# Batch 0 of the last loop: half of the quad sums on GpSimd, and the order of residuals and squares

## The chip, the cores and the metric

The kernel is one program on one core of a Trainium2 chip. The core has five engines that run side by side and meet only at semaphores: TensorE (PE, matrix products), VectorE (DVE), ScalarE (ACT), GpSimd (POOL) and SyncE (SP, which here only starts transfers). Transfers between the large memory and the core's own memory (SBUF) run on 16 DMA engines; they are started from SP and from ACT. The metric is the device time of one execution in microseconds (us), as the median of several runs.

## The reference

`x` is (8, 128, 256, 256) float32. Two layers are computed:

```python
x = x + _L0_conv_ref(_gn(x), ...)   # layer 0
x = x + _L1_conv_ref(_gn(x), kernel)  # layer 1: 4x4 depthwise blur of the group-normed x
# layer 0, inside:
ll, lh, hl, hh = haar_dwt(x)                     # to half resolution, 4*128 channels
h = gelu(batchnorm(conv1x1(cat(ll, lh, hl, hh), w_c1, b_c1)))       # 128 channels
o = dwconv3x3(h, dw_w, dw_b); o = layernorm_chw(o); o = conv1x1(o, pw1)
h = conv1x1(gelu(o), pw2) + h                                       # u below
h = gelu(batchnorm(conv1x1(h, w_c2, b_c2)))      # 4*128 channels: LL, LH, HL, HH
# haar_idwt: y00 = (ll+lh+hl+hh)/2, y01 = (ll+lh-hl-hh)/2, y10 = (ll-lh+hl-hh)/2, y11 = (ll-lh-hl+hh)/2
```

## The kernel before

Channels lie on the 128 partitions. The program has three stages. The first reads `x` for statistics and makes the first 1x1 convolution. The second makes the depthwise and pointwise convolutions and leaves `u_scratch`. The third, `phase_tail`, starts its first x load at 2587.4 us and is the only one that the change touches.

`phase_tail` works on units. A unit is 8 image rows of one batch, 32 units to a batch. For each unit `k` of batch `b`:

- SP (`load_unit`) loads `u_in` (256 KB) and the matching piece of `x` into one of four slots of `x_tile` (1024 KB). A slot is loaded again when the `y` stored from it four units earlier has landed.
- PE (`convolve`, L1289) makes four products of 128x512, one for each Haar band, into the PSUM tiles `conv_psum` 0 to 3. Each float32 product shows as two MATMUL records.
- ACT (`gelus`, L1397) applies batch norm and gelu: bands 0 and 2 to `gelu_out` (two buffers), bands 1 and 3 in place in PSUM.
- DVE (`pairs`, L1162) makes four pair sums of 128x512, each from one SBUF and one PSUM operand, into `pair_sums`, which has one buffer. Its semaphore also frees PSUM bands 1 and 3 for PE.
- DVE (`quads`, L1170) makes two quad sums of 128x1024 from `pair_sums`, both operands in SBUF: the one with ADD gives the even columns of `quad_sums`, the one with SUBTRACT the odd columns. Each row is written with a step of two elements.
- DVE (`residual`, L1177) makes `x_tile = 0.5 * quad_sums + x_tile` over 128x2048, both in SBUF.
- ACT (`finish`) starts the store of the `x_tile` slot to `y_scratch` (L1404, 1024 KB) and squares the slot for the second group norm (L1408).

Batch `b-1` is blurred beside the units of batch `b`. `split` on ACT makes `y_hi` and `y_centred_tile`, `rests` on GpSimd (L1106) makes `y_lo`, `blur` on PE multiplies both with band matrices, and `take` on DVE (L1184, one PSUM and one SBUF operand) adds the result to `y_tile`. The body is written out for the phases FIRST (batch 0), SECOND (batch 1), MIDDLE (a hardware loop over batches 2 to 7), DRAIN and END. In FIRST there is nothing to blur, and GpSimd has no instruction. The order on each engine is the order in which the Python code writes it. In every phase up to MIDDLE the order on DVE is pairs(k), quads(k), residual(k), and on ACT gelus(k), finish(k-1).

`y_tile` has eight slots of 128x2048. In FIRST none of them is in use; the first loads into them are made in SECOND.

Of the kernel before, what the change touches and what calls it, by code (L numbers as in the profile page):

```python
# [8 lines left out]
ALU = mybir.AluOpType  # L9
# [5 lines left out]
H2, W2 = H // 2, W // 2  # L15
# [871 lines left out]
UNITS = H // ROWS3  # L887
# [16 lines left out]
FIRST, SECOND, MIDDLE, DRAIN, END = range(5)  # L904


def group_at(b, phase, k, lag):

    if phase == FIRST or (phase == SECOND and k < lag) or (phase == END and k >= lag):
        return None  # L910
    return b * NG - NG + (k - lag)


def phase_tail(nc, kp, wc2, x, u_d, y_d, out):
# [4 lines left out]
    with ExitStack() as ctx:  # L919
        sb = lambda name, shape, dt=F32: ctx.enter_context(nc.sbuf_tensor(name, shape, dt))  # L920
        ps = lambda name, shape: ctx.enter_context(nc.psum_tensor(name, shape, F32))
        sem = kp["sem"]
        w = sb("w_conv2", [128, 4 * C])
# [6 lines left out]
        x_t = sb("x_tile", [128, XS, XW])  # L930
        u_t = sb("u_in", [128, US, UW])
        g_t = sb("gelu2_out", [128, 2, 2, UW])
        sums_t = sb("pair_sums", [128, 4, UW])
        d_t = sb("quad_sums", [128, XW])
# [3 lines left out]
        y_t = sb("y_tile", [128, YS, 2, GRP, W])  # L938
# [12 lines left out]
        spread_s = sb("gn2_seam_spread", [128, 2, NQ])  # L951
        rest_n = sb("rests_of_partition", [128, 1])
        rest_i = sb("rests", [1, 1], mybir.dt.int32)
        cv = [ps(f"conv2_psum{s}", [128, BANK]) for s in range(4)]
        bl = [ps(f"blur_psum{t}", [128, GRP, W]) for t in range(2)]
        small = cv[2]
# [12 lines left out]
        s_ge = sem("gelu2_done")  # L969
        s_s1 = sem("pair_sums_done")  # L970
        s_s2 = sem("quad_sums_done")
        s_y = sem("y_ready")
        s_sq = sem("y_squared")
        s_yst = [sem(f"y_stored{i}") for i in range(XS)]
# [26 lines left out]
        yr = y_d.rearrange("b c h w -> (b c) h w")  # L1001
        ov = out.rearrange("b c h w -> (b c) h w")
        block = ctx.enter_context(nc.Block())

        def phases(engine, body):
            body(0, FIRST)
# [77 lines left out]
        @block.gpsimd  # L1084
        def _(pool):

            for y in (y_hi, y_lo):
                for cols in (slice(0, 2), slice(2 + W, PADW)):
                    pool.memset(y[:, :, :, cols].bitcast(F32), 0.0).then_inc(s_set, 1)
            for y in (seam_hi, seam_lo):  # L1090
                for cols in (slice(0, 2), slice(2 + W, PADW)):
                    pool.memset(y[:, cols].bitcast(F32), 0.0).then_inc(s_set, 1)
            pool.wait_ge(s_v, 5)
            nc.gpsimd.tensor_tensor(t4[:, 2, :], t4[:, 1, :], neg_half[:, 0:4], ALU.pow).then_inc(s_rs, 1)

            def rests(b, phase, k):
                g = k - LAG_SPLIT
                h = g % 2
                at = b * NG - NG + g
                pool.wait_ge(s_hi, at + 1)  # L1100
                pool.wait_ge(s_c, at + 1)
                if not (phase == SECOND and g < 2):
                    pool.wait_ge(s_t, 2 * at - 2)
                for t in range(2):
                    part = slice(t * GRP, (t + 1) * GRP)
                    nc.gpsimd.tensor_tensor(  # L1106
                        y_lo[:, h, part, 2:2 + W], y_c[:, part, :],
                        y_hi[:, h, part, 2:2 + W].bitcast(F32), ALU.subtract).then_inc(s_lo, 1)
                if g % QUAD == 2:
                    pool.wait_ge(s_sc, b * NQ - NQ + g // QUAD + 3)  # L1110
                    nc.gpsimd.tensor_tensor(seam_lo[:, 2:2 + W], seam_c[:],
                                            seam_hi[:, 2:2 + W].bitcast(F32), ALU.subtract).then_inc(s_slo, 1)

            def body(b, phase):
                for k in range(LAG_SPLIT if phase == END else UNITS):
                    if group_at(b, phase, k, LAG_SPLIT) is not None:
                        rests(b, phase, k)
                    if k == 1 and SECOND <= phase <= DRAIN:
                        pool.wait_ge(s_gve, b)
                        nc.gpsimd.tensor_tensor(st[:, 8:9], st[:, 7:8], neg_half[:, 0:1], ALU.pow).then_inc(s_grs, 1)  # L1120

            phases(pool, body)

        @block.vector
        def _(dve):
# [28 lines left out]
            dve.wait_ge(s_p, 5)  # L1154
            nc.vector.tensor_copy(rest_i[:], cv[0][0:1, 0:1]).then_inc(s_ready, 1)

            def pairs(b, k):
                for p in range(2):

                    dve.wait_ge(s_ge, b * (4 * UNITS) + 4 * k + 2 * p + 2 + 4)  # L1160
                    for m, op in enumerate((ALU.add, ALU.subtract)):
                        ins = nc.vector.tensor_tensor(sums_t[:, 2 * m + p, :], g_t[:, k % 2, p, :], cv[2 * p + 1][:], op)  # L1162
                    ins.then_inc(s_s1, 1)

            def quads(b, k):
# [4 lines left out]
                    ins = nc.vector.tensor_tensor(dv[:, :, e], sv[:, :, 0], sv[:, :, 1], op)  # L1170
                ins.then_inc(s_s2, 1)

            def residual(b, k):
                i = k % XS
                dve.wait_ge(s_x[i], b * (16 * UNITS // XS) + 16 * (k // XS) + 16)
                dve.wait_ge(s_s2, b * UNITS + k + 1)
                nc.vector.scalar_tensor_tensor(x_t[:, i, :], d_t[:], 0.5, x_t[:, i, :],  # L1177
                                               ALU.mult, ALU.add).then_inc(s_y, 1)

            def take(b, k, t):  # L1180
# [14 lines left out]
            def body(b, phase):  # L1195
                c = b - 1
                done = SECOND <= phase <= DRAIN
                gl = Chain(dve, s_gl, c * LINKS_GN)
                for k in range(LAG_BLUR if phase == END else UNITS):
                    if phase <= MIDDLE:  # L1200
                        pairs(b, k)
                    if done and k == 1:

                        dve.wait_ge(s_sq, b * UNITS + XS)
# [17 lines left out]
                        ins.then_inc(s_gsp, 1)  # L1222
                    if phase <= MIDDLE:
                        quads(b, k)
                        residual(b, k)
                    if done and k == 1:
                        dve.wait_ge(s_gp, b * 2 - 1)
                        gl.link(nc.vector.tensor_copy(st[:, 5:6], small[:, 0:1]))
# [15 lines left out]
                    if group_at(b, phase, k, LAG_BLUR) is not None:  # L1244
# [3 lines left out]
                        take(b, k, 1)  # L1248

            phases(dve, body)  # L1250

        @block.tensor
# [126 lines left out]
        def _(act):  # L1379
# [20 lines left out]
            def finish(b, k):  # L1400

                i = k % XS
                act.wait_ge(s_y, b * UNITS + k + 1)
                act.dma_start(yv[bass.ds(b, 1), :, k * XW:(k + 1) * XW].rearrange("b c n -> c (b n)"),  # L1404
                              x_t[:, i, :]).then_inc(s_yst[i], 16)

                act.wait_ge(s_sq, b * UNITS + k + XS)
                nc.scalar.activation(junk[:], x_t[:, i, :], ACT.Square, bias=neg_gm[:, bass.ds(b, 1)],  # L1408
                                     accum_out=y_sq[:, bass.ds(b, 1), k]).then_inc(s_sq, 1)
# [31 lines left out]
            def body(b, phase):  # L1441
                for k in range(LAG_SPLIT if phase == END else UNITS):
                    if phase <= MIDDLE:
                        gelus(b, k)
                    if k >= 1 and phase <= MIDDLE:
                        finish(b, k - 1)
                    elif k == 0 and SECOND <= phase <= DRAIN:
                        finish(b - 1, UNITS - 1)
                    if group_at(b, phase, k, LAG_SPLIT) is not None:
                        split(b, phase, k)  # L1450
                        if (k - LAG_SPLIT) % QUAD == 2:
                            split_seam(b, phase, k)
# [50 lines left out]
```

## Time and profile before

| | |
|---|---|
| median of 3 runs | 5678.01 us (5661.07 to 5681.14) |
| the profiled execution's own time | 5670.85 us |
| its span in the trace | 5669.0 us |
| TensorE's mean granted clock | 0.97 of full speed |
| FIRST, first unit's pair sums to batch 1's first pair sums | 2603.59 to 2834.11 us |
| busy over the span: PE, DVE, ACT, POOL | 92%, 77%, 66%, 36% |

The span runs from the first to the last record of the trace; the execution's own time is 1.85 us longer. Shares of busy time are means over three stages and say little about one of them. For FIRST the stretch from 2600 to 2834 us has to be read by itself.

### The profile page before, as it was taken

How to read it: one execution, taken by the hardware profiler on the slowest of the kernel's cores; microseconds unless marked ns; L12 is line 12 of the kernel's file. 1: busy time of each engine (PE TensorE's matmuls, PEld its weight loads, DVE VectorE, ACT ScalarE, POOL GpSimd, SP SyncE). 2: the span in 40 equal slices, each digit the busy share in tenths (PEclk: the TensorE clock that was granted, in tenths of full speed). 3: DMA queues.
4: the chain of work that ended last, by engine and by line, in shares of the span. 5: the costliest groups of instructions: out<-in, count | busy, mean ns of one | idle time of the engine just before them, and what ended most of it. 6: DMA issues, size and time to landing. Idle time of an engine off the chain costs nothing. (4 is left out here: it accounts for less than half of the span.)

```text
span 5669.0 us, 67162 instructions
## 1 busy us (share of the span) xinstructions
PE 5201.0 (92%) x18136; PEld 3151.9 (56%) x18136; DVE 4380.2 (77%) x5325; ACT 3721.8 (66%) x5012; POOL 2066.9 (36%) x1397
## 2 busy tenths in 40 slices
PE   2888888986999999997699999999999999999999
PEld 1333333332555555563256666676666666666777
DVE  8555555428999999966988888888888888888833
ACT  0333333346777777755678787787887878878744
POOL 0000000018777777730023333333333333333354
PEclk9999999998999999998899999999999999999999
DMA  9999999842333333326999999999999999999986
GB/s 369 375 374 377 379 378 375 343 142 72 107 110 108 107 106 106 108 86 240 330 384 404 396 399 401 390 399 383 389 394 388 399 389 398 398 392 393 397 291 228
DMA packets 829594, 1729.83 MB, mean 305 GB/s; under 512 B 50064, under 2 KB 587152, under 8 KB 718608
## 3 DMA queue, kind: packets, MB, share of 16 engines
q1 hardware_dynamic: 755472, 1389.81, 66.6%
q10 hardware_dynamic: 73728, 335.58, 14.4%
q8 instruction: 148, 2.42, 0.2%
q14 instruction: 246, 2.02, 0.1%
HBM read 1050.95 MB, written 674.23 MB: 304 GB/s over the span
## 5 line engine op out<-in xcount | busy, mean ns | idle before, releaser
L1106 POOL TENSOR_TENSOR y_lo<-y_centred_tile,y_hi 128x1024 fp32r<-128x1024 f32 x512 | 1040.8, 2054 | 1724.5 <-ACT y_centred_tile L1427 1410.4
L1306 PE MATMUL blur_psum<-y_hi,band_hi 128*128 128x512 f32 x4096 | 1127.8, 417 | 8.8 <-DVE y_tile L1184 7.4
L1289 PE MATMUL conv_psum<-u_in,w_conv 128*128 128x512 f32 x2048 | 971.2, 618 | 109.1 <-DVE pair_sums L1162 85.2
L1306 PE MATMUL blur_psum<-y_lo,band_hi 128*128 128x512 f32 x4096 | 1041.8, 396 | 7.5 <-POOL y_lo L1106 7.0
L1306 PEld LDWEIGHTS blur_psum<-y_hi,band_hi 128*128 128x128 f32 x4096 | 764.9, 188 | 278.8 <-issue 100.9
L1162 DVE TENSOR_TENSOR pair_sums<-gelu_out,conv_psum 128x512 f32<-128x512 f32 x1024 | 653.5, 684 | 305.7 <-ACT conv_psum L1397 299.8
L1306 PEld LDWEIGHTS blur_psum<-y_lo,band_hi 128*128 128x128 f32 x4096 | 769.4, 188 | 200.7 <-POOL y_lo L1106 16.5
L1184 DVE SCALAR_TENSOR_TENSOR y_tile<-blur_psum,rstd_all,y_tile 128x1024 f32<-128x1024 f32 x512 | 639.6, 1277 | 159.4 <-PE blur_psum L1306 152.2
L1397 ACT ACTIVATE gelu_out<-conv_psum,bn_shift,bn_scale 128x512 f32<-128x512 f32 x512 | 397.5, 776 | 515.3 <-PE conv_psum L1289 493.7
L1289 PEld LDWEIGHTS conv_psum<-u_in,w_conv 128*128 128x128 f32 x2048 | 398.1, 197 | 559.7 <-issue 407.1
L608 POOL TENSOR_TENSOR tap_products<-tap_products 128x512 f32<-128x512 f32 x512 | 653.8, 1277 | 43.0 <-ACT tap_products L869 6.5
L869 ACT ACTIVATE tap_products<-h_ring,vectors 128x512 f32<-128x512 f32 x768 | 499.0, 712 | 215.0 <-POOL depthwise_out L612 215.0
L313 DVE BATCH_NORM_STATS2 x_stats<-x_resident 128x6 f32<-128x512 f32 x640 | 395.2, 681 | 294.7 <-DMA x_resident<-x 293.5
L1170 DVE TENSOR_TENSOR quad_sums<-pair_sums 128x1024 f32<-128x1024 f32 x512 | 604.8, 1223 | 8.4
L1177 DVE SCALAR_TENSOR_TENSOR x_tile<-quad_sums,x_tile 128x2048 f32<-128x2048 f32 x256 | 596.9, 2332 | 13.9
L1425 ACT ACTIVATE y_hi<-y_tile,neg_mean_all 128x2048 fp32r<-128x2048 f32 x256 | 513.3, 2005 | 137.6 <-POOL y_lo L1106 137.6
L374 PE MATMUL z_psum<-x_resident,w_folded 128*128 128x512 f32 x1280 | 600.1, 625 | 0.5 <-ACT z_psum L399 0.5
L657 DVE SCALAR_TENSOR_TENSOR dw_psum<-h_ring,vectors,dw_psum 128x512 f32<-128x512 f32 x768 | 578.0, 753 | 25.2 <-PE dw_psum L761 6.7
L395 ACT ACTIVATE z_tile<-z_psum,z_bias 128x512 f32<-128x512 f32 x256 | 176.0, 687 | 638.5 <-DMA z_scratch<-z_tile 428.3
L761 PE MATMUL dw_psum<-h_ring,tap_diagonals 128*128 128x512 f32 x1024 | 500.9, 612 | 65.3 <-DVE depthwise_out L657 54.9
L1408 ACT ACTIVATE junk<-x_tile,neg_group_mean 128x2048 bf16<-128x2048 f32 x256 | 511.7, 1999 | 59.8 <-DVE x_tile L1177 56.6
L1427 ACT ACTIVATE y_centred_tile<-y_tile,neg_mean_all 128x2048 f32<-128x2048 f32 x256 | 509.7, 1991 | 0.0
(166 smaller groups left out, 5451.4 us busy)
## 6 DMA issues: line engine op xcount, KB each, us to landing
x_tile<-x SPq DMA_DIRECT2D x256, 1024.0 KB, 10.0
y_scratch<-x_tile ACTq DMA_DIRECT2D x256, 1024.0 KB, 8.4
y_tile<-y_scratch SPq DMA_DIRECT2D x512, 512.0 KB, 10.9
out<-y_tile SPq DMA_DIRECT2D x512, 512.0 KB, 10.1
x_stream<-x SPq DMA_DIRECT2D x192, 1024.0 KB, 11.4
x_resident<-x SPq DMA_DIRECT2D x160, 1024.0 KB, 11.1
z_scratch<-z_tile ACTq DMA_DIRECT2D x256, 256.0 KB, 7.2
z_in<-z_scratch SPq DMA_DIRECT2D x256, 256.0 KB, 2.8
```

The source lines that it names most:

```text
L374: ins = nc.tensor.matmul(zp[q % ZP][:, half * BANK:(half + 1) * BANK], w_f[:, p, :], px[:, p // 2, p % 2, rows, :], start=(p == 0), stop=( ...
L608: nc.gpsimd.tensor_tensor(pr[:, 0, :], pr[:, 0, :], pr[:, n, :], ALU.add).then_inc(s_add, 1)
L657: taps.link(nc.vector.scalar_tensor_tensor(to.rearrange("p (r c) -> p r c", c=W2), tap(k, e), V[:, V_DWW + k:V_DWW + k + 1], acc.rearrange ...
L1106: nc.gpsimd.tensor_tensor(y_lo[:, h, part, 2:2 + W], y_c[:, part, :], y_hi[:, h, part, 2:2 + W].bitcast(F32), ALU.subtract).then_inc(s_lo, 1)
L1162: ins = nc.vector.tensor_tensor(sums_t[:, 2 * m + p, :], g_t[:, k % 2, p, :], cv[2 * p + 1][:], op)
L1170: ins = nc.vector.tensor_tensor(dv[:, :, e], sv[:, :, 0], sv[:, :, 1], op)
L1177: nc.vector.scalar_tensor_tensor(x_t[:, i, :], d_t[:], 0.5, x_t[:, i, :], ALU.mult, ALU.add).then_inc(s_y, 1)
L1184: nc.vector.scalar_tensor_tensor(y_t[:, g % YS, t], bl[t][:], rs_b[:, bass.ds(n, 1)], y_t[:, g % YS, t], ALU.mult, ALU.add).then_inc(s_ev, 1)
L1289: nc.tensor.matmul(cv[s][:], w[:, s * C:(s + 1) * C], u_t[:, k % US, :], start=True, stop=True).then_inc(s_mm, 1)
L1306: ins = nc.tensor.matmul(bl[t][:, 2 * c:2 * c + 2, :], wt[:, kw, :], y[:, h, ch:ch + 2, kw:kw + W], start=(m == 0 and kw == 0), stop=(m == ...
L1408: nc.scalar.activation(junk[:], x_t[:, i, :], ACT.Square, bias=neg_gm[:, bass.ds(b, 1)], accum_out=y_sq[:, bass.ds(b, 1), k]).then_inc(s_s ...
L1425: nc.scalar.activation(y_hi[:, h, :, 2:2 + W], src, ACT.Identity, bias=nm_b[:, bass.ds(n, 1)]).then_inc(s_hi, 1)
```

## The change

Only FIRST changes. The steps are:

1. GpSimd makes the odd quad sums of batch 0's 32 units. DVE makes the even ones (`even_quads`) and then signals `quad_sums_done`; GpSimd waits for that and signals `odd_sums_done`.
2. `pair_sums` and `quad_sums` get a second buffer each, in the unused slots 4 and 5 of `y_tile`; units alternate between them.
3. DVE's order becomes pairs(k), residual(k-1), even_quads(k). Before residual(k-1) it waits for `odd_sums_done` of unit k-1. After unit 31 there is one more residual by itself.
4. ACT's order becomes gelus(k), finish(k-2), with finish(30) added at the end of FIRST; finish(31) stays in SECOND, behind the gelus of batch 1's first unit.

```diff
+        sums_of = [sums_t[:], y_t[:, 4].rearrange("p t c w -> p (t c w)").rearrange("p (s n) -> p s n", s=4)]
+        quads_of = [d_t[:], y_t[:, 5].rearrange("p t c w -> p (t c w)")]
...
+        s_q1 = sem("odd_sums_done")
...
+        def quad_views(k):
+            dv = quads_of[k % 2].rearrange("c (i a j e) -> c a e i j", a=2, e=2, j=W2)
+            sv = sums_of[k % 2].rearrange("c (a p) (i j) -> c a p i j", p=2, j=W2)
+            return dv[:, :, 0], dv[:, :, 1], sv[:, :, 0], sv[:, :, 1]
...
 @@ gpsimd, body(b, phase)
+                    if phase == FIRST:
+                        pool.wait_ge(s_s2, k + 1)
+                        _, odd, first, second = quad_views(k)
+                        nc.gpsimd.tensor_tensor(odd, first, second, ALU.subtract).then_inc(s_q1, 1)
...
 @@ vector
+            def even_quads(k):
+                dve.wait_ge(s_s1, 2 * k + 2 + 4)
+                even, _, first, second = quad_views(k)
+                nc.vector.tensor_tensor(even, first, second, ALU.add).then_inc(s_s2, 1)
...
+                if phase == FIRST:
+                    for k in range(UNITS + 1):
+                        if k < UNITS:
+                            pairs(0, k, sums_of[k % 2])
+                        if k >= 1:
+                            dve.wait_ge(s_q1, k)
+                            residual(0, k - 1, quads_of[(k - 1) % 2])
+                        if k < UNITS:
+                            even_quads(k)
+                    return
...
 @@ scalar, body(b, phase)
-                    if k >= 1 and phase <= MIDDLE:
+                    if phase == FIRST:
+                        if k >= 2:
+                            finish(b, k - 2)
+                        if k == UNITS - 1:
+                            finish(b, k - 1)
+                    elif k >= 1 and phase <= MIDDLE:
                         finish(b, k - 1)
```

How this moves instructions is shown by what stands in a row on an engine. First VectorE at the start of the last loop, before (L1162 is pairs, L1170 quads, L1177 residual; conv2_psum is what the trace calls conv_psum):

```order
L1162 TENSOR_TENSOR pair_sums<-gelu2_out,conv2_psum1 128x512 x2
L1162 TENSOR_TENSOR pair_sums<-gelu2_out,conv2_psum3 128x512 x2
L1170 TENSOR_TENSOR quad_sums<-pair_sums 128x2x4x128 x2
L1177 SCALAR_TENSOR_TENSOR x_tile<-quad_sums,x_tile 128x2048
L1162 TENSOR_TENSOR pair_sums<-gelu2_out,conv2_psum1 128x512 x2
```

and the same place now (L1176 is pairs, L1191 even_quads, L1197 residual; y_tile is the second buffer):

```order
L1176 TENSOR_TENSOR pair_sums<-gelu2_out,conv2_psum1 128x512 x2
L1176 TENSOR_TENSOR pair_sums<-gelu2_out,conv2_psum3 128x512 x2
L1191 TENSOR_TENSOR quad_sums<-pair_sums 128x2x4x128
L1176 TENSOR_TENSOR y_tile<-gelu2_out,conv2_psum1 128x512 x2
L1176 TENSOR_TENSOR y_tile<-gelu2_out,conv2_psum3 128x512 x2
L1197 SCALAR_TENSOR_TENSOR x_tile<-quad_sums,x_tile 128x2048
L1191 TENSOR_TENSOR y_tile<-y_tile 128x2x4x128
L1176 TENSOR_TENSOR pair_sums<-gelu2_out,conv2_psum1 128x512 x2
```

Each unit has one quad sum instead of two on VectorE, and a unit's residual stands behind the next unit's pair sums.

At the end of FIRST, where batch 1 begins, VectorE has now:

```order
L1191 TENSOR_TENSOR quad_sums<-pair_sums 128x2x4x128
L1176 TENSOR_TENSOR y_tile<-gelu_out,conv_psum 128x512 x4
L1197 SCALAR_TENSOR_TENSOR x_tile<-quad_sums,x_tile 128x2048
L1191 TENSOR_TENSOR y_tile<-y_tile 128x2x4x128
L1197 SCALAR_TENSOR_TENSOR x_tile<-y_tile,x_tile 128x2048
L1176 TENSOR_TENSOR pair_sums<-gelu_out,conv_psum 128x512 x4
L1184 TENSOR_TENSOR quad_sums<-pair_sums 128x2x4x128 x2
```

The last residual of batch 0 follows its quad sum with no pair sums between the two; from L1184 on the order is the old one.

## Rows read from the trace of the kernel before

**Rows 1.** The page's busy times over the whole span

```profile
PE 5201.0 (92%) x18136; PEld 3151.9 (56%) x18136; DVE 4380.2 (77%) x5325; ACT 3721.8 (66%) x5012; POOL 2066.9 (36%) x1397
```

**Rows 2.** Windows of batch 0's units, of loops before and behind; columns as in the first line

```profile
core 0: us, PE busy (x) PEld busy (x) DVE busy (x) ACT busy (x) POOL busy (x), PEclk, DMA share, GB/s
700.00:800.00 100.00, 93.34 (x196) 38.74 (x197) 56.76 (x92) 33.23 (x85) 0.00 (x0) 0.93 0.99 397
...
2740.00:2780.00 40.00, 26.69 (x45) 10.54 (x46) 39.27 (x41) 27.83 (x40) 0.00 (x0) 0.83 0.91 319
3000.00:3100.00 100.00, 100.00 (x377) 69.58 (x376) 86.85 (x84) 81.62 (x85) 36.00 (x20) 1.00 1.05 404
```

**Rows 3.** Timeline of one unit of FIRST: start us, length us, engine, line, operation

```profile
2709.73 2.29 DVE L1177 SCALAR_TENSOR_TENSOR x_tile<-quad_sums,x_tile 128x2048 f32<-128x2048 f32 x1
2711.94 2.47 DVE L1162 TENSOR_TENSOR pair_sums<-gelu_out,conv_psum 128x512 f32<-128x512 f32 x4
...
2712.44 2.00 ACT L1408 ACTIVATE junk<-x_tile,neg_group_mean 128x2048 bf16<-128x2048 f32 x1 [2.35 <-DVE x_tile L1177]
...
2713.27 3.70 PE L1289 MATMUL conv_psum<-u_in,w_conv 128*128 128x512 f32 x8 [3.48 <-DVE pair_sums L1162]
...
2714.45 2.38 DVE L1170 TENSOR_TENSOR quad_sums<-pair_sums 128x1024 f32<-128x1024 f32 x2
...
2716.53 0.75 ACT L1397 ACTIVATE conv_psum<-conv_psum,bn_shift,bn_scale 128x512 f32<-128x512 f32 x1
2716.93 2.29 DVE L1177 SCALAR_TENSOR_TENSOR x_tile<-quad_sums,x_tile 128x2048 f32<-128x2048 f32 x1
```

**Rows 4.** Durations by line: pairs, quads (whole trace), residuals, products; min/median/max ns

```profile
L1162 DVE TENSOR_TENSOR pair_sums<-gelu_out,conv_psum x122: 680/681/684, 2612.5 to 2828.7; 128x512 f32<-128x512 f32 x122
...
L1170 DVE TENSOR_TENSOR quad_sums<-pair_sums x512: 1216/1225/1249, 2606.6 to 5365.8; 128x1024 f32<-128x1024 f32 x171
...
L1177 DVE SCALAR_TENSOR_TENSOR x_tile<-quad_sums,x_tile x32: 2291/2292/2293, 2609.1 to 2831.9; 128x2048 f32<-128x2048 f32 x32
...
L1289 PE MATMUL conv_psum<-u_in,w_conv x248: 592/592/1222, 2612.6 to 2831.4; 128*128 128x512 f32 x124
```

**Rows 5.** Timeline of VectorE: batch 0's first quad sums, batch 1's first pair sums

```profile
2606.63 2.36 DVE L1170 TENSOR_TENSOR quad_sums<-pair_sums 128x1024 f32<-128x1024 f32 x2
...
2834.11 2.47 DVE L1162 TENSOR_TENSOR pair_sums<-gelu_out,conv_psum 128x512 f32<-128x512 f32 x4
```

**Rows 6.** Durations of GpSimd's two-input subtraction, whole trace; min/median/max ns

```profile
L1106 POOL TENSOR_TENSOR y_lo<-y_centred_tile,y_hi x512: 1987/2000/4047, 2868.4 to 5655.4; 128x1024 fp32r<-128x1024 f32 x171
```

**Rows 7.** Timeline: one hand-over from VectorE to GpSimd, one back

```profile
2304.91 0.75 DVE L657 SCALAR_TENSOR_TENSOR depthwise_out<-h_ring,vectors,dw_psum 128x512 f32<-128x512 f32 x1
...
2305.81 1.27 POOL L612 TENSOR_TENSOR depthwise_out<-depthwise_out,tap_products 128x512 f32<-128x512 f32 x1 [0.37 <-DVE depthwise_out L657]
...
2596.22 1.02 POOL L1094 TENSOR_TENSOR four_columns<-four_columns,neg_half 128x4 f32<-128x4 f32 x1 [9.21 <-DVE four_columns L1145]
...
2597.28 0.17 DVE L1151 TENSOR_TENSOR bn_scale<-four_columns,vectors 128x4 f32<-128x4 f32 x1 [0.33 <-POOL four_columns L1094]
```

**Rows 8.** Timeline: y_lo beside pairs, and y_lo beside a residual, last loop

```profile
2868.40 3.97 POOL L1106 TENSOR_TENSOR y_lo<-y_centred_tile,y_hi 128x1024 fp32r<-128x1024 f32 x2 [17.99 <-ACT y_centred_tile L1427]
...
2869.67 2.62 DVE L1162 TENSOR_TENSOR pair_sums<-gelu_out,conv_psum 128x512 f32<-128x512 f32 x4 [1.12 <-ACT conv_psum L1397]
...
3210.78 6.65 POOL L1106 TENSOR_TENSOR y_lo<-y_centred_tile,y_hi 128x1024 fp32r<-128x1024 f32 x2 [6.07 <-ACT y_centred_tile L1427]
3211.60 3.97 DVE L1177 SCALAR_TENSOR_TENSOR x_tile<-quad_sums,x_tile 128x2048 f32<-128x2048 f32 x1
```

**Rows 9.** DMA issues in FIRST: KB each, median us from issue to landing

```profile
y_scratch<-x_tile ACTq DMA_DIRECT2D x32, 1024.0 KB, 6.2
x_tile<-x SPq DMA_DIRECT2D x31, 1024.0 KB, 6.3
u_in<-u_scratch SPq DMA_DIRECT2D x32, 256.0 KB, 5.3
```

More of the change, by code:

```diff
@@ L1155, in _, with pairs @@
             nc.vector.tensor_copy(rest_i[:], cv[0][0:1, 0:1]).then_inc(s_ready, 1)
-            def pairs(b, k):
+            def pairs(b, k, sums):
                 for p in range(2):
@@ L1161, in pairs @@
                     for m, op in enumerate((ALU.add, ALU.subtract)):
-                        ins = nc.vector.tensor_tensor(sums_t[:, 2 * m + p, :], g_t[:, k % 2, p, :], cv[2 * p + 1][:], op)
+                        ins = nc.vector.tensor_tensor(sums[:, 2 * m + p, :], g_t[:, k % 2, p, :], cv[2 * p + 1][:], op)
                     ins.then_inc(s_s1, 1)
@@ L1171, in quads, with residual @@
                 ins.then_inc(s_s2, 1)
-            def residual(b, k):
+            def even_quads(k):
+                dve.wait_ge(s_s1, 2 * k + 2 + 4)
+                even, _, first, second = quad_views(k)
+                nc.vector.tensor_tensor(even, first, second, ALU.add).then_inc(s_s2, 1)
+            def residual(b, k, quads):
                 i = k % XS
@@ L1176, in residual @@
                 dve.wait_ge(s_s2, b * UNITS + k + 1)
-                nc.vector.scalar_tensor_tensor(x_t[:, i, :], d_t[:], 0.5, x_t[:, i, :],
+                nc.vector.scalar_tensor_tensor(x_t[:, i, :], quads, 0.5, x_t[:, i, :],
                                                ALU.mult, ALU.add).then_inc(s_y, 1)
@@ L1198, in body @@
                 gl = Chain(dve, s_gl, c * LINKS_GN)
+                if phase == FIRST:
[8 more added lines that the diff above has]
+                    return
                 for k in range(LAG_BLUR if phase == END else UNITS):
                     if phase <= MIDDLE:
-                        pairs(b, k)
+                        pairs(b, k, sums_t)
                     if done and k == 1:
@@ L1224, in body @@
                         quads(b, k)
-                        residual(b, k)
+                        residual(b, k, d_t[:])
                     if done and k == 1:
```

## The prediction, made before the changed kernel ran

> **What bounds the kernel now.** I began with the page's busy times [rows 1]: PE is busy for 92% of the span and DVE for 77%. That would say that relief for DVE is worth nothing, but it is a mean over three stages. The windows [rows 2] take it apart. From 3000 to 3100 us PE is busy for all of the time; from 2740 to 2780 us, in FIRST, DVE is busy for 39.27 of 40 us and PE for 26.69. The timeline of one unit [rows 3] then shows who waits for whom. DVE runs residual (2709.73), pairs (2711.94), quads (2714.45), residual (2716.93) with no idle time noted, while PE waits 3.48 us for pair_sums and ACT 2.35 us for x_tile. So DVE alone sets the pace. One unit takes 2716.93 - 2709.73 = 7.20 us, and from the first quad sums to batch 1's first pair sums [rows 5] it is 2834.11 - 2606.63 = 227.48 us for 31 steps from unit to unit and one end. That stretch is what I forecast; the loops before and behind keep their instructions.
>
> **DVE's unit after the change.** I use steps from start to start, not lengths, since the instructions overlap. Residual to pairs is 2711.94 - 2709.73 = 2.21 us [rows 3]. Four pairs end 2.47 us after their start and one lasts 0.68 us [rows 3, 4], so one step is (2.47 - 0.68) / 3 = 0.60 and four are 2.39 us. Two quads end after 2.38 us and one lasts 1.23 [rows 3, 4], so one step is 1.15 us. Before, quads begin 2.51 us after pairs and residual 2.48 us after quads; both contain about 0.1 to 0.2 us in which DVE waits for its own last result. In the new order neither residual(k-1) nor even_quads(k) needs the instruction right in front of it, so these gaps go too. DVE's own unit is 2.39 + 2.21 + 1.15 = 5.75 us. Removed: one quad of 1.15 to 1.24 us and 0.2 to 0.3 us of gaps.
>
> **The new wait.** Residual(k-1) waits for GpSimd's odd sum. Behind it on DVE stand even_quads(k) and pairs(k+1), for which PE and ACT wait. The loop is: even sum 1.23 [rows 4]; hand-over to GpSimd 0.15 (L657 ends at 2305.66, L612 starts at 2305.81 [rows 7]); odd sum D; hand-over back 0.04 (2597.24 to 2597.28 [rows 7]); residual 2.21. That is 3.63 + D. No row shows GpSimd writing with a step of two elements. The nearest has the same shape and operand count, y_lo, with a median of 2.00 us, a lowest value of 1.99 and a longest of 4.05 [rows 6]. 1.99 and 4.05 are my ends, and I take 2.00, since elements and operands are the same. The loop is then 5.63 us, hidden under DVE's 5.75 by 0.12 us. If D were over 2.12 us each further 0.1 us would cost 0.1 us a unit.
>
> **Does GpSimd disturb DVE?** At 3210.78 two y_lo need 6.65 us together instead of 3.97, and the residual that starts among them at 3211.60 lasts 3.97 us instead of 2.29 [rows 4, 8]. So GpSimd and a residual hold each other up. In the new order they cannot meet: residual waits for the odd sum, and the odd sum for the even one. What runs beside the odd sum is pairs, with one operand in PSUM. From 2869.67 to 2872.29 four pairs ran beside two y_lo: 2.62 us for the pairs instead of 2.47, and 3.97 us for the two y_lo, as elsewhere. I take nothing, and carry the 0.15 us, which for a unit on DVE's pace would make 5.90 us, inside the next term. The Trainium skill (SBUF — State Buffer, section "SBUF: two separate sides") calls the port pair an exclusive lock between GpSimd and DVE work with two SBUF inputs, held for the whole instruction. That speaks against handing a sum to GpSimd beside a busy DVE; by its wording pairs stay outside the lock, and the sum by it is the same as by rows 8, which agree.
>
> **ACT and PE.** ACT's unit is square to last gelu, 2712.44 to 2717.28, or 4.84 us [rows 3], and about 0.4 us for the store issue: 5.2 us, under 5.75. The store of unit k-1 is issued behind gelus(k+1); those end close to the end of residual(k-1), so the store is not later than now by more than some tenths. PE's four products take 3.70 us at full clock [rows 3]. From the end of pairs(k) the band-3 product (0.93) and gelu (0.75) need 1.7 us, and pairs(k+1) wants them after 2.21 + 1.15 + 1.20 = 4.6 us: 2.9 us of slack. But the granted clock is 0.83 there [rows 2], that is, for a third of the time at 1.2 GHz instead of 2.4, and a product's record then lasts 1222 instead of 592 ns [rows 4]. A unit that falls wholly into it needs 1.2 + 1.2 us for each of three products behind pairs' first half, 7.3 + 0.75 - 1.2 = 6.9 us, 2.3 us late. Spells are mostly shorter than a unit, so I carry 0 to 0.1 us a unit, inside the next term.
>
> **The DMA engines.** This is what is late next. A unit moves 1024 + 1024 + 256 KB [rows 9] = 2.36 MB, at 7.20 us 328 GB/s. At 5.75 us it would be 410 GB/s. The fastest long stretches are 404 GB/s at a share of 1.05 and 397 GB/s at 0.99 [rows 2]. In FIRST a share of 0.91 carried only 319 GB/s; scaled to 1.05 that is 368. So the unit is bounded by 2.36/404 = 5.84 us on one side and 2.36/368 = 6.41 us on the other. The ends are near each other and I take the middle, 6.1 us. Latency does not bind: store and load have medians of 6.2 and 6.3 us [rows 9], with the residual some 15 us against 4 x 6.1 = 24 us for four slots.
>
> **Sum.** 31 x 6.1 + 3.63 + 2.00 = 194.7 us; the last part is the end of FIRST, where even sum, odd sum and residual stand one behind the other with nothing between, and costs 5.63 us once. Saved: 227.48 - 194.7 = 32.8 us. Against the profiled execution's own 5670.85 us (span 5669.0) this gives 5638 us. That execution is 7 us under the median of the runs, 5678.01, and between the fastest, 5661.07, and it; I keep its level. With the ends 5.84 and 6.41 us the saving is 40.8 and 23.2 us: 5630 and 5648.
>
> **Rivals.**
> - DVE's own pace holds, DMA follows at 410 GB/s: 31 x 5.75 + 5.63 = 183.9, 43.6 us saved, 5627 us. For it: DVE is the only engine without idle time. Against: no long window reached 410. Chance 0.20.
> - The DMA engines saturate as soon as their share is 1.00 at FIRST's own yield: 319/0.91 = 351 GB/s, 6.73 us a unit, 214.3 us, 13 us saved, 5658 us. For it: the poor yield in FIRST. Against: shares of 1.05 and 404 GB/s. Chance 0.14. The Trainium skill (SBUF — State Buffer, section "A bandwidth-pool intuition that's wrong (but worth ruling out)") gives about 358 GB/s between HBM and a core; an estimate by it is 6.59 us a unit and 5653 us. The trace's 404 GB/s over 100 us disagrees.
> - TensorE's low clock catches whole units, one in three late by the 2.3 us above: 6.5 us a unit, 207 us, 20 us saved, 5650 us. For it: 0.83. Against: PE and ACT have slack, and the spells now cost DVE nothing. Chance 0.08.
> - Slower: the odd sum on GpSimd is slow, by its stepped writes or because pairs do shut it out. It decides from D = 227.48/32 - 3.63 = 3.48 us. At the longest 4.05 us [rows 6] the unit is 7.68 us, 245.8 us in all, 18 us lost, 5689 us. For it: one operation of unknown write pattern. Against: a median of 2.00 us in 512 cases. Chance 0.06.
> - The saving appears in FIRST and batch 1 gives it back, since its y loads and gn2 columns wait for batch 0's last stores and squares: 5670 us. Against: these are in the same distance from the last residual as now. Chance 0.04.
>
> **How the numbers follow.** The forecast (5.84 to 6.41 us a unit) has 0.48. What a measurement of this kernel can tell from no change is about 0.5%, 28 us. The forecast passes that up to 6.25 us a unit, about four fifths of its chance, 0.38; with the first rival, faster is 0.58. The rest of the forecast and the second, third and fifth rival are 0.36; slower 0.06. The range runs from 5627 less some scatter, 5621, to the second rival's 5658 and some scatter, 5664.
>
> **What would show it.** In the changed profile: batch 0's residuals 5.8 to 6.4 us apart; GpSimd's new line at 2.0 to 2.1 us, starting 0.15 us behind the even sum; DVE with small idle times put down to x loads, where the DMA share is about 1.05; no idle time before residual put down to GpSimd. The forecast is wrong if residual waits for GpSimd in each unit, if DVE waits for ACT's gelus in most, or if the distance stays near 7.2 us.

## The result

| kernel | median, us | runs | ratio to the kernel before, 95% interval |
|---|---|---|---|
| before | 5669.81 (5657.97 to 5681.14) | 13 | |
| changed | 5656.42 (5651.93 to 5669.07) | 13 | 0.998 (0.9973 to 0.9988) |

The change saves 13 us, a gain that is clear of noise, and I had forecast 33. The time lies inside my range, but the gain is only 0.4 of the forecast one. The page and the rows below come from the slowest of the 13 executions (5669.07 us); a second trace is read near the end of the experiments.

The page's first lines of the changed kernel:

```profile
span 5667.0 us, 67162 instructions
...
PE 5208.1 (92%) x18136; PEld 3155.5 (56%) x18136; DVE 4342.4 (77%) x5293; ACT 3725.1 (66%) x5012; POOL 2141.6 (38%) x1429
```

VectorE has 38 us less work than in [rows 1] (4342.4 against 4380.2) and GpSimd 75 us more (2141.6 against 2066.9). So the work moved as intended. These are the windows of batch 0, columns as in [rows 2]:

```profile
2680.00:2720.00 40.00, 25.65 (x40) 10.00 (x40) 30.47 (x33) 25.70 (x36) 13.02 (x6) 0.74 0.87 317
2720.00:2760.00 40.00, 25.87 (x49) 10.16 (x50) 34.74 (x36) 29.40 (x43) 14.80 (x7) 0.91 0.93 344
```

In these two windows DVE is busy for 30.47 and 34.74 of 40 us, where it was busy for 39.27 [rows 2]. DVE got less to do and in part just idles. The DMA engines are at a share of 0.87 and 0.93, about as before (0.91); whether they could carry more can't be read from these rows, and the experiments have to say it. The durations, as in [rows 4] and [rows 6]:

```profile
L1129 POOL TENSOR_TENSOR quad_sums<-pair_sums x16: 2354/2363/2383, 2608.9 to 2813.9; 128x1024 f32<-128x1024 f32 x16
...
L1197 DVE SCALAR_TENSOR_TENSOR x_tile<-quad_sums,x_tile x16: 2284/2285/2293, 2611.3 to 2821.4; 128x2048 f32<-128x2048 f32 x16
```

The odd sum takes 2.36 to 2.37 us and not the 2.00 of y_lo. Next come one unit of the changed kernel that does not run as planned (from 2697.30 us) and one that does (from 2720.64 us). The lines are from the timeline of DVE and GpSimd, with one of PE's products; the bracket is the idle time before, and who ended it:

```profile
2697.30 2.29 DVE L1197 SCALAR_TENSOR_TENSOR x_tile<-y_tile,x_tile 128x2048 f32<-128x2048 f32 x1
...
2700.41 9.81 PE L1319 MATMUL conv_psum<-u_in,w_conv 128*128 128x512 f32 x16 [7.22 <-DMA u_in<-u_scratch]
...
2705.01 1.28 DVE L1176 TENSOR_TENSOR y_tile<-gelu_out,conv_psum 128x512 f32<-128x512 f32 x2 [4.29 <-ACT conv_psum L1427]
...
2708.82 2.29 DVE L1197 SCALAR_TENSOR_TENSOR x_tile<-quad_sums,x_tile 128x2048 f32<-128x2048 f32 x1
...
2720.64 2.29 DVE L1197 SCALAR_TENSOR_TENSOR x_tile<-quad_sums,x_tile 128x2048 f32<-128x2048 f32 x1
...
2722.85 1.22 DVE L1191 TENSOR_TENSOR y_tile<-y_tile 128x1024 f32<-128x1024 f32 x1
...
2723.99 2.48 DVE L1176 TENSOR_TENSOR pair_sums<-gelu_out,conv_psum 128x512 f32<-128x512 f32 x4
2724.15 2.37 POOL L1129 TENSOR_TENSOR y_tile<-y_tile 128x1024 f32<-128x1024 f32 x1 [3.54 <-DVE y_tile L1191]
...
2726.55 2.29 DVE L1197 SCALAR_TENSOR_TENSOR x_tile<-y_tile,x_tile 128x2048 f32<-128x2048 f32 x1
```

From 2720.64 to 2726.55 residuals are 5.91 us apart. GpSimd's sum starts at 2724.15 and ends at 2726.52, and the residual starts at 2726.55: it waits for GpSimd. At 2697.30 and 2708.82 they are 11.52 us apart. There DVE stood idle for 4.29 us in the middle of its pair sums, waiting for ACT, because PE had stood idle for 7.22 us for u_in. These are the waits of batch 0 (engine, line, whom for: us in total, times, longest):

```profile
PE conv_psum L1319 <- DMA u_in<-u_scratch: 67.5, 22, 7.2
...
ACT gelu_out L1427 <- PE conv_psum L1319: 63.7, 27, 17.2
DVE y_tile L1176 <- ACT conv_psum L1427: 32.1, 22, 4.3
```

Before, PE waited in the same stretch for DVE's pair_sums and never for u_in:

```profile
PE conv_psum L1289 <- DVE pair_sums L1162: 81.8, 31, 3.9
```

From the first quad sum (2607.57) to batch 1's first pair sums (2829.52) it is 221.95 us, against 227.48 [rows 5]. The 31 distances between residuals lie between 5.89 and 11.52 us and are 6.97 in the mean; before, all were 7.18 to 7.20.

**Where the u_in load hangs.** The same place with SP and ACT (SPq and ACTq are DMA issues):

```profile
2688.93 0.33 SPq L1034 DMA_DIRECT2D x_tile<-x  x1
...
2689.42 0.34 ACTq L1434 DMA_DIRECT2D y_scratch<-x_tile  x1
...
2690.09 1.99 ACT L1438 ACTIVATE junk<-x_tile,neg_group_mean 128x2048 bf16<-128x2048 f32 x1
...
2692.20 0.33 SPq L1029 DMA_DIRECT2D u_in<-u_scratch  x1
...
2697.91 0.33 SPq L1034 DMA_DIRECT2D x_tile<-x  x1
2698.28 0.43 SPq L1029 DMA_DIRECT2D u_in<-u_scratch  x1
```

The square that starts at 2690.09 ends at 2692.1, and at 2692.20 SP issues the u_in load: `load_unit` waits for `y_squared` of unit k-4 before it loads u_in for unit k. The load lands 8.2 us later and PE starts at 2700.41. The next u_in load was free by its square at about 2696.9, but SP stood at the x load before it, which waits for the y store of 2689.42 to land, until 2697.91; u_in followed at 2698.28. The diff does not touch `load_unit`. But it moves the squares and the stores a unit back against the gelus, and both are what SP waits for. The kernel had this wait on `y_squared` before the change too; the description of `load_unit` ahead of the prediction leaves it out.

### The profile page after: what moved, and what is told of

Same layout as the page of the kernel before. It is cut to its first block and busy times, and to the rows that moved or that the text cites. A ratio compares the mean times of both kernels' runs of the same rounds, so it can differ in the third digit from the quotient of the medians.

```text
span 5667.0 us, 67162 instructions
## 1 busy us (share of the span) xinstructions
PE 5208.1 (92%) x18136; PEld 3155.5 (56%) x18136; DVE 4342.4 (77%) x5293; ACT 3725.1 (66%) x5012; POOL 2141.6 (38%) x1429
## 5 line engine op out<-in xcount | busy, mean ns | idle before, releaser
L1176 DVE TENSOR_TENSOR pair_sums<-gelu_out,conv_psum 128x512 f32<-128x512 f32 x960 | 614.2, 684 | 308.7 <-ACT conv_psum L1427 308.6
L1197 DVE SCALAR_TENSOR_TENSOR x_tile<-quad_sums,x_tile 128x2048 f32<-128x2048 f32 x240 | 560.2, 2334 | 11.0
L1184 DVE TENSOR_TENSOR quad_sums<-pair_sums 128x1024 f32<-128x1024 f32 x448 | 529.1, 1223 | 7.3
## 6 DMA issues: line engine op xcount, KB each, us to landing
out<-y_tile SPq DMA_DIRECT2D x512, 512.0 KB, 10.4
```

What stands on the lines that cost most here:

```text
L1176: ins = nc.vector.tensor_tensor(sums[:, 2 * m + p, :], g_t[:, k % 2, p, :], cv[2 * p + 1][:], op)
L1197: nc.vector.scalar_tensor_tensor(x_t[:, i, :], quads, 0.5, x_t[:, i, :], ALU.mult, ALU.add).then_inc(s_y, 1)
```

## The experiments

Theory A: the u_in load now hangs on a square and a store that come later, so load, products, gelus and square form a loop that is longer than DVE's unit. Rival B: the DMA engines cannot carry a unit's 2.36 MB faster. Rival C: TensorE's low clock makes the products late. "Stretch" is always from the first quad sum to batch 1's first pair sums, "distance" the mean of the 31 distances between residuals; both are read from VectorE's timeline of each run.

| kernel | distance, us | stretch, us | time, us |
|---|---|---|---|
| before | 7.19 | 227.48 | 5669.81 (13 runs) |
| changed | 6.97 | 221.95 | 5656.42 (13 runs) |
| changed, a second trace | 6.66 | 212.26 | 5663.65 (one) |
| u_in waits for the product, old place | 6.75 | 214.99 | 5655.16 (6 runs) |
| u_in one unit ahead, waits for the square | 6.40 | 204.32 | 5651.34 (one) |
| u_in one unit ahead, waits for the product | 6.05 | 193.37 | 5636.76 (4 runs) |
| u_in two units ahead, waits for the product | 5.91 | 189.23 | 5635.87 (4 runs) |
| the same, even sum ahead of the residual | 5.81 | 190.14 | 5628.18 (4 runs) |

**u_in one unit ahead, waiting for the product.** In batch 0 SP loads u_in for k+1 before it waits for x's slot of unit k:

```diff
-                sp.wait_ge(s_sq, b * UNITS + k + 1)
-                sp.dma_start(u_t[:, k % US, :], ...).then_inc(s_u[k % US], 16)
+                def load_u(m):
+                    if m >= US:
+                        sp.wait_ge(s_mm, 4 * (m - US) + 4 + 16)
+                    sp.dma_start(u_t[:, m % US, :], ...).then_inc(s_u[m % US], 16)
+                if phase == FIRST:
+                    if k == 0:
+                        load_u(0)
+                    if k + 1 < UNITS:
+                        load_u(k + 1)
+                    sp.wait_ge(s_sq, k + 1)
...
```

From batch 1 on the u_in load stays as it was.

> The changed kernel, with one edit in batch 0: SP issues the load of u_in for unit k+1 ahead of unit k's x load, and it waits for the product of unit k-3 and no longer for a square. In the changed kernel residuals are 6.97 us apart in the mean and PE waits some 60 us for u_in. Theory A (the u_in load hangs on the square, which now comes one unit later, so load, products, gelus, square form a loop): the wait of PE for u_in goes, residuals are 5.9 to 6.1 us apart, batch 0 takes 187 to 195 us from its first quad sum to batch 1's first pair sums, the time falls to 5625 to 5640 us. Rival B (the 16 DMA engines can't carry 2.36 MB in under about 6.7 us here): the wait only moves to the x loads, residuals stay 6.6 to 7.0 us apart, the time stays within 8 us of the changed kernel's. Rival C (TensorE's low clock makes the products late): waits of ACT and DVE for products remain, 6.5 us or more.

Measured: 0.9935 (0.9918 to 0.9952) of the kernel before, 5636.76 us, distance 6.05, stretch 193.37 us. PE's waits in batch 0 are now:

```profile
PE conv_psum L1333 <- DMA u_in<-u_scratch: 33.7, 16, 5.8
```

Distance, stretch and time are what theory A gave. Its "the wait goes" came only half true: 33.7 us of 67.5 are left. B and C as the cause of the 6.97 us fall: the same bytes are carried, and the same products made, in 6.05 us a unit. The median is 20 us lower than that of the changed kernel. C has a part all the same. These are PE's products of two units in a row, in the changed kernel:

```profile
2655.22 5.09 PE L1319 MATMUL conv_psum<-u_in,w_conv 128*128 128x512 f32 x8 [3.81 <-DMA u_in<-u_scratch]
2661.63 3.70 PE L1319 MATMUL conv_psum<-u_in,w_conv 128*128 128x512 f32 x8 [1.31 <-DMA u_in<-u_scratch]
```

The granted clock is 0.82 from 2620 to 2700 us, between 1.2 and 2.4 GHz by turns. In this trace a unit's products that meet the lower one last 5.1 to 5.4 us instead of 3.70. As long as PE waits for u_in they stand in the loop of theory A and lengthen it. How much of the 6.97 us that makes was not separated.

**The two halves of that edit.** Only the semaphore, in the old place on SP:

```diff
+                if phase == FIRST:
+                    if k >= US:
+                        sp.wait_ge(s_mm, 4 * (k - US) + 4 + 16)
+                else:
                     sp.wait_ge(s_sq, b * UNITS + k + 1)
                 sp.dma_start(u_t[:, k % US, :], ...).then_inc(s_u[k % US], 16)
+                if phase == FIRST:
+                    sp.wait_ge(s_sq, k + 1)
```

> The changed kernel, with the u_in load of batch 0 waiting for the product of unit k-4 instead of the square, but in its old place on SP, behind the x load of unit k-1, which waits for the y store of unit k-5. Theory A: a longer loop is left (gelus(k-3), y store 7.0 us, x load issued, u_in 6.4 us, products and gelus 4.4 us: 18 us for 3 units): 6.0 to 6.4 us apart, and time 5630 to 5648 us, between the changed kernel and the one with u_in ahead. Rival B: as the changed kernel, 6.6 to 7.0 us.

Measured: 0.9974 (0.9961 to 0.9986), 5655.16 us, distance 6.75, stretch 214.99 us: as the changed kernel. That is what rival B gave and a miss for theory A's 6.0 to 6.4 us. My 18 us for the loop through the store were too few; in this run SP waited 163 us in all for y stores. Only the order, with the wait for the square kept:

```diff
                     if m >= US:
-                        sp.wait_ge(s_mm, 4 * (m - US) + 4 + 16)
+                        sp.wait_ge(s_sq, m + 1)
```

> The changed kernel with u_in of unit k+1 issued ahead of x of unit k in batch 0, but still behind the square of unit k-3. The kernel with the product's semaphore and the old place brought 6.75 us between residuals, the one with both edits 6.05. Theory A has two loops: one through the square (store issue and square 2.7, u_in 6.4, products and gelus 4.4 us: 13.5 us for two units, 6.75 us), one through the y store in front of it on SP (about 18 us for three units and more with waits). With the square's wait kept, the first loop stays: 6.6 to 7.1 us apart, stretch 210 to 225 us, PE waits 40 us or more for u_in. Rival: if SP's order alone was the cause, 6.0 to 6.2 us.

Measured: distance 6.40, stretch 204.32 us, 5651.34 us in a single run. Its waits:

```profile
PE conv_psum L1333 <- DMA u_in<-u_scratch: 59.9, 26, 5.0
```

The distance is between both expectations and a miss for either. With this trace's median landing of 5.8 us instead of 6.4 the loop through the square gives (2.7 + 5.8 + 4.4) / 2 = 6.45 us, close to the 6.40. It is one trace, and the stretches of the changed kernel's two traces differ by 10 us (221.95 and 212.26). Still, with either wait left in place the distance stays at 6.40 or more, against 6.05 without both: both have to go.

**The same edit in the kernel before.**

> The kernel before, with the u_in load of batch 0 ahead in the same way. All theories: PE never waited for u_in there, DVE sets the pace; residuals stay 7.19 us apart and batch 0's stretch 227 to 228 us. If it gets shorter, the u_in load already cost something before.

Measured: distance 7.18, stretch 227.35 us, 5673.90 us in a single run. The u_in load cost nothing as long as DVE took 7.19 us.

**u_in two units ahead.**

```diff
                     if k == 0:
                         load_u(0)
-                    if k + 1 < UNITS:
-                        load_u(k + 1)
+                        load_u(1)
+                    if k + 2 < UNITS:
+                        load_u(k + 2)
```

> The changed kernel with u_in in batch 0 loaded two units ahead of x instead of one. With one unit ahead residuals were 6.05 us apart in the mean (25 of 31 at 5.9) and PE still waited 34 us for u_in. Theory A (the rest was the u_in load too): 5.91 to 5.95 us apart, batch 0's stretch 189 to 190 us, 3 to 4 us less than with one ahead, time 5630 to 5637 us. Rival B (the DMA engines are full at a share of 0.99): the 6.05 us stay, and the waits show up at x loads.

Measured: 0.9938 (0.9921 to 0.9955), 5635.87 us, distance 5.91 with no exception, stretch 189.23 us. Its u_in loads, with the time to landing:

```profile
L1031 SPq DMA_DIRECT2D u_in<-u_scratch x26: 327/734/1832, 2603.4 to 2757.8; - x26
...
DMA to landing us min/median/max: 3.5/10.4/12.7
```

The same window in the kernel before and in this one, columns as in [rows 2]:

```profile
2610.00:2780.00 170.00, 108.83 (x189) 42.10 (x190) 166.78 (x167) 116.77 (x166) 0.00 (x0) 0.86 0.88 319
...
2610.00:2780.00 170.00, 116.43 (x223) 44.63 (x222) 167.24 (x174) 142.54 (x199) 68.80 (x29) 0.92 1.00 389
```

Its waits of PE:

```profile
PE conv_psum L1334 <- DVE pair_sums L1191: 26.4, 15, 2.2
PE conv_psum L1334 <- DVE y_tile L1191: 26.2, 15, 2.2
...
PE conv_psum L1334 <- DMA u_in<-u_scratch: 3.7, 1, 3.7
```

PE waits for u_in once, for 3.7 us. The u_in load now takes a median of 10.4 us to land, and but for that once nobody waits. The DMA engines move 389 GB/s at a share of 1.00, against 319 at 0.88 in the same window of the kernel before: B falls for good.

**The even sum ahead of the residual**, so that the residual meets GpSimd's sum:

```diff
-                        if k >= 1:
-                            dve.wait_ge(s_q1, k)
-                            residual(0, k - 1, quads_of[(k - 1) % 2])
                         if k < UNITS:
                             even_quads(k)
+                        if k >= 1:
+                            dve.wait_ge(s_q1, k)
+                            residual(0, k - 1, quads_of[(k - 1) % 2])
```

> As the one with u_in two units ahead, and on VectorE the even sum(k) stands in front of residual(k-1) instead of behind it, so that the residual can meet the odd sum(k). If GpSimd and a two-SBUF-input instruction of VectorE shut each other out and VectorE is first, the odd sum starts only when the residual ends, 2.2 us later than now, and runs beside the pair sums; the unit is then 1.15 + 2.21 + 2.39 = 5.75 us up to 5.9 us, batch 0's stretch 184 to 189 us. If GpSimd is first each time, the residual lasts 4.6 us or starts 2.4 us late and the unit is 8.1 to 8.3 us, stretch 260 us. If they did not disturb each other, the odd sum would start 0.1 us behind the even sum, with 5.75 us a unit.

Measured: 0.9928 (0.9909 to 0.9948), 5628.18 us, the fastest median of all, though its interval overlaps the one above. One unit of it (timeline of DVE and GpSimd):

```profile
2716.88 2.28 DVE L1212 SCALAR_TENSOR_TENSOR x_tile<-quad_sums,x_tile 128x2048 f32<-128x2048 f32 x1
2717.05 4.36 POOL L1144 TENSOR_TENSOR y_tile<-y_tile 128x1024 f32<-128x1024 f32 x1 [1.50 <-DVE y_tile L1206]
...
2719.09 2.47 DVE L1191 TENSOR_TENSOR pair_sums<-gelu_out,conv_psum 128x512 f32<-128x512 f32 x4
...
2721.59 1.23 DVE L1206 TENSOR_TENSOR quad_sums<-pair_sums 128x1024 f32<-128x1024 f32 x1
...
2722.74 2.29 DVE L1212 SCALAR_TENSOR_TENSOR x_tile<-y_tile,x_tile 128x2048 f32<-128x2048 f32 x1
2722.90 4.36 POOL L1144 TENSOR_TENSOR quad_sums<-pair_sums 128x1024 f32<-128x1024 f32 x1 [1.50 <-DVE quad_sums L1206]
```

The residual starts in front of GpSimd's sum and keeps its 2.28 us. The sum's record is 4.36 us long instead of 2.37. It ends at 2721.41, 2.25 us after the residual (2719.16), so it looks as if the sum stood still while the residual ran and then worked beside the pair sums. The expectation had it start later; the record starts at once and is longer. The unit is 2722.74 - 2716.88 = 5.86 us. The 0.11 us over DVE's own 5.75 are the gap between pairs and the even sum, which again stands right behind them (2721.59 - 2719.09 = 2.50 us instead of 2.39). GpSimd's sum is off the path, since it has until after the next even sum. The stretch is no shorter than the 189.23 us above. At its end PE waits 10.5 us for batch 1's first u_in load, and the last residual and batch 1's first pair sums are 5.20 us apart (2779.95 to 2785.15) instead of 2.21; at its start the first residual comes 1.1 us later. So the two traces of batch 0 don't show the 8 us between the medians.

**GpSimd's sum in the old order.** DVE keeps pairs, even sum, wait, residual; ACT finishes one unit behind, by the same edit as in the next experiment:

```diff
+                    for k in range(UNITS):
+                        pairs(0, k, sums_of[k % 2])
+                        even_quads(k)
+                        dve.wait_ge(s_q1, k + 1)
+                        residual(0, k, quads_of[k % 2])
```

> The changed kernel, in which DVE and ACT keep the old order: pairs(k), even sum(k), wait for the odd sum, residual(k), and finish one unit behind the gelus. The odd sum (2.37 us in the changed kernel) then stands in DVE's row: 2.39 + 1.22 + 0.08 + 2.37 + 0.03 + 2.21 = 8.3 us a unit, batch 0's stretch 262 to 268 us, 35 to 40 us more than the kernel before. Rival: if GpSimd and DVE disturbed each other beyond that, or not at all, it would be 9 us or more, or near 7.2.

Measured: distance 8.41, stretch 266.63 us, 5715.31 us. The residual waits 2.46 us for GpSimd in each unit, so it has to stand behind the next unit's pair sums. In this run VectorE does nothing beside the odd sum:

```profile
L1129 POOL TENSOR_TENSOR quad_sums<-pair_sums x16: 2344/2350/2357, 2610.2 to 2862.5; 128x1024 f32<-128x1024 f32 x16
```

It lasts 2.35 us even so. The pair sums beside it are thus not the reason for its length in the changed kernel.

**ACT's old order in the changed kernel.**

```diff
-                    if phase == FIRST:
-                        if k >= 2:
-                            finish(b, k - 2)
-                        if k == UNITS - 1:
-                            finish(b, k - 1)
-                    elif k >= 1 and phase <= MIDDLE:
+                    if k >= 1 and phase <= MIDDLE:
```

> The changed kernel with ACT's old order: store and square of unit k-1 behind the gelus of unit k, as before. The square then waits for residual(k-1), which now stands behind pairs(k); gelus(k+1) stand behind the square, and pairs(k+1) wait for them: 2.39 + 0.2 + 2.29 + 0.5 + 2.1 + 1.6 = 9.1 us a unit, 8.8 to 9.3, batch 0's stretch 278 to 292 us, 50 to 65 us more than the kernel before. So the two-unit lag, whatever it does to the u_in load, is what makes the rest possible. Rival: if the lag were not needed, 5.9 to 6.5 us, and the u_in wait gone.

Measured: distance 8.68, stretch 274.83 us, 5714.38 us, slightly under my bounds. No wait for u_in is left, but ACT waits 122 us for residuals. So the two-unit lag is needed as well. That it also brings the u_in wait is shown by the next run and not by this one, in which the units are slower anyway.

**The new order without GpSimd.** VectorE makes both sums (one line added in `even_quads`, GpSimd's instruction and the wait for it taken out). ACT stays two units behind.

> The changed kernel without GpSimd: VectorE makes both quad sums, in the new order (pairs(k), residual(k-1), both sums(k)), with the new buffers and ACT two units behind. VectorE's own unit is 2.39 + 2.21 + 2.31 = 6.91 us, 0.28 less than before, from gaps that the order takes away. Theory A: the loop through square, u_in load (6.4 us), products and gelus allows 6.75 us in two-unit turns and is now and then the later one, so 6.9 to 7.3 us apart and some PE waits for u_in; stretch 218 to 230 us. Rival: if only GpSimd's part makes PE wait for u_in, 6.91 us throughout and no wait for u_in, 218 us.

Measured: distance 6.92 (28 of 31 at 6.86 to 6.89), stretch 221.36 us, 5660.27 us. The order alone gives 0.3 us a unit, as my term for DVE's gaps said, and PE waits 59 us for u_in here too, mostly hidden behind DVE's 6.86. GpSimd has no part in that wait.

**Why GpSimd's sum takes 2.37 us.** First both sums are written without a step, in the kernel with u_in one unit ahead. The diff shows GpSimd's sum; VectorE's even sum gets the same views and writes the first half. Nothing puts the columns back in order, so batch 0's output columns stand in another order than the reference's:

```diff
+                        sums = sums_of[k % 2].rearrange("c (a p) n -> c a p n", p=2)
+                        odd = quads_of[k % 2].rearrange("c (h a n) -> c h a n", h=2, a=2)[:, 1]
+                        nc.gpsimd.tensor_tensor(odd, sums[:, :, 0], sums[:, :, 1], ALU.subtract).then_inc(s_q1, 1)
```

> The kernel with u_in one unit ahead, with both quad sums of batch 0 written without the step of two elements (even sums to the first half of quad_sums, odd ones to the second; batch 0's output columns are therefore in another order than the reference's). The odd sum on GpSimd took 2.37 us instead of the 2.00 us that y_lo has. If the stepped writes are the reason: 1.99 to 2.05 us, and the unit falls to VectorE's 5.75 us plus at most 0.1, stretch 184 to 190 us. If not (the reads, or rows of 128 elements), 2.3 to 2.4 us and 5.9 us a unit.

Then `odd.bitcast(F32R)` as output, in the kernel with u_in two units ahead:

> The kernel with u_in two units ahead, with the odd quad sum of GpSimd written as fp32r, the type that y_lo is written in. With both sums written without a step, the odd sum still took 2.37 us, against 2.00 us for y_lo, so the step is not the reason. If the type of the output is: 1.99 to 2.05 us, the wait of DVE's residual goes and VectorE's own 5.75 to 5.8 us a unit shows, stretch 184 to 187 us. If not (what is left is how the two inputs lie): 2.37 us and 5.91 us again, stretch 189 us.

Measured: 2.36 to 2.37 us in both, distances 6.10 and 5.91, stretches 194.84 and 189.22 us, 5635.40 and 5635.12 us in a single run each. Neither the step nor the output's type is the reason, nor are the pair sums beside it (2.35 us without them). How the two inputs lie or the length of their rows were not tried; the reason stays open.

**A second trace of the changed kernel.**

> The changed kernel once more, for a second trace. Its profiled execution took 5669.07 us and batch 0's stretch 221.95 us, while the median of 13 runs is 5656 us. Theory A: the loop through the u_in load is made of transfer latencies that vary, so the distances between residuals again jump between 5.9 and 8 to 12 us in another pattern, with PE's waits for u_in at 40 to 80 us; an execution near the median has a stretch of about 205 to 218 us. Rival: the same pattern and a stretch of 222 us, with the difference elsewhere.

Measured: distances again between 5.90 and 11.48 us, but at other units, mean 6.66, stretch 212.26 us, PE waits 62.5 us for u_in. So the saving in batch 0 itself varies: 5.5 us in the first trace and 15.2 in the second. That fits a median 13 us lower.

## Why the prediction was right or wrong

- **DVE sets the pace, and its own unit becomes 5.75 us.** The steps were right, the pace was not. The gaps were real: without GpSimd, 6.86 us were measured for 2.39 + 2.21 + 2.31 = 6.91. But in the changed kernel DVE waits, and no run reached 5.75; the nearest was 5.85 us, with the even sum ahead of the residual.
- **The loop 3.63 + D.** The mechanism was right, D too small: 2.37 us instead of 2.00. By my formula that gives 6.00 us; measured are 5.91, mostly because the hand-over to GpSimd took 0.08 us (2724.07 to 2724.15) and not 0.15. I had written that it costs something from D = 2.12 on. Against the 5.75 it cost 0.16 us a unit, 5 us in all, once u_in was out of the way. The price was inside my ends, not at the median that I took.
- **GpSimd and pairs do not disturb each other.** Right: four pairs last 2.47 to 2.48 us beside GpSimd's sum, and the sum 2.37 us beside them and 2.35 without them. The Trainium skill's rule of the exclusive pair (SBUF — State Buffer, section "SBUF: two separate sides") has the one that starts first keep the ports and the other wait. The trace with the even sum ahead of the residual agrees: the residual started first and kept its 2.28 us, and the sum ended 2.25 us behind it, about the time that it takes alone.
- **ACT and PE: "so the store is not later than now by more than some tenths".** This is the step that failed, with its second half under the DMA engines, "Latency does not bind". I measured the moved `finish` by its store's distance to the residual, which held (the residual of 2691.40 ends at 2693.68, its store is issued at 2693.72), and by the four slots of x. I did not ask what else waits for it, and so put the wait of PE for u_in at nothing without a reason. SP waits for the square before it loads u_in, so the square's distance to the gelus of its own unit, one unit more than before, is taken from the time in which u_in must land. I even listed the queue behind residual on DVE, and not SP's behind the square. The rows were there: store issue and square 2.7 us, u_in's 5.3 us to land [rows 9], products and gelus 4.4 us are 12.4 us for two units, 6.2 us a unit at the median landing, with nothing in reserve for later ones. With the old order the same 12.4 us had three units, 4.1 us each, under DVE's 7.19. The changed kernel's traces have median landings of 6.4 and 5.9 us, which make 6.75 and 6.5 us a unit; measured were 6.97 and 6.66. The rest was not taken apart: it holds the u_in load's place behind x on SP and the products at low clock. It cost 28 us in the first trace (221.95 against 193.37 with one unit ahead) and 19 in the second.
- **The DMA engines, 6.1 us a unit.** Wrong as a bound. With u_in out of the way they carried a unit in 5.91 and even 5.86 us, close to my lower end of 5.84; the scaled 6.41 us was wrong, since the share of 0.91 was no measure of how full they were. That my sum of 194.7 us lies so near the 193.37 us of the repaired kernel is two errors that cancel: a DMA term too large, and a GpSimd term too small plus a rest of the u_in wait. It is luck, too, that the time of the changed kernel lies inside the range: the lower gains in it, down to the second rival's 6.73 us a unit, stood for full DMA engines, and the measured 6.97 and 6.66 us came from the u_in loop.
- **The low clock.** With u_in two units ahead it costs nothing: at a granted clock of 0.92 all distances are 5.90 to 5.92 us. In the changed kernel, where PE waits for u_in, it had a part of unknown size.
- **The end of FIRST, 5.63 us.** 5.90 in the trace (2823.62 to 2829.52), with the exposed wait of 2.47 us for GpSimd; the difference is the longer odd sum again.

## What to carry to other kernels

When an instruction is moved back in one engine's order, list every semaphore that it and its DMA raise, and for each the load that waits for it; a prefetch that shares a "slot is free" signal with something else is moved too. Give each load the signal of its own last reader, and issue small loads, on which the first engine of the chain waits, ahead of large ones in the same queue. Where an engine's pace falls, compare the new pace with the time that the whole way round every loop takes, not with the engines' busy times.

## What the runs showed of the hardware

- GpSimd's subtraction of 128x1024 float32 took 2.35 to 2.37 us here, whatever the step or type of the output and with or without VectorE's pair sums beside it, and 2.00 us as y_lo. Why is open.
- Where VectorE's residual, with two SBUF inputs, started 0.17 us ahead of GpSimd's sum, the sum's record was 4.34 to 4.36 us long instead of 2.37, and the residual lost nothing (2.28 us).
- The loop through transfers gave no steady pace: 5.9 us, interrupted by 6.3 to 11.5 us, in another pattern in each of the two traces, where the unit on DVE's pace varied by 0.02 us.
- The DMA engines' share was 0.88 at 319 GB/s and 1.00 at 389 GB/s in the same window of batch 0: the GB/s grew more than the share.
